# A two-layer recurrent block on one core: the high half of x1 moved a step ahead, the fp32 state moved to PSUM

## The chip, the cores and the metric

The kernel runs on one core of a Trainium2 chip. The metric is the device time of one execution in microseconds; the number given is the median over several runs. The engines are TensorE (PE: matrix products, PEld: its weight loads), VectorE (DVE), ScalarE (ACT), GpSimd (POOL) and SyncE (SP, which here only issues DMAs). Each engine works through its own instructions in order, and they meet through semaphores.

## What is computed

The input is x with 32 sequences of 64 steps and 256 features. There are two layers, and each adds to x the output of a feed-forward part that is fed by a recurrence over the 64 steps.

```python
# layer 0
gate  = sigmoid(h @ Wh.T + z_t @ Wz.T + b);  h = tanh(h * leak + gate * z_t)
x1    = x + experts(hs)          # 8 experts, the best 2 per token
# layer 1
h     = tanh(x1_t @ Wx + b + h @ Wh)
out   = x1 + bitlinear(gelu(bitlinear(hs, w1)), w2)   # ternary weights, 8-bit rows
```

In bitlinear each row of the activations is scaled by 127 over its largest absolute value and rounded; the weights are -1, 0 or 1 times a scale.

## The kernel before, in words

There are 2048 tokens in order of time, 128 to a tile, so that one tile holds four steps of the recurrence (32 sequences each) and there are 16 tiles. Float32 numbers that go into TensorE are split into two fp16 numbers, a high and a low one (the rest), and a product is made of three: high by high, low by high, high by low.

The program has three stages: the first recurrence (to about 125 us), 39 tiles of expert work (to about 286 us), and the second recurrence, in which the change lies. In the third stage every engine runs its own function tanh_tile(k, par) for tile k, with par = k % 2. Within it, four steps s = 0 to 3 follow one another, and behind the recurrence's part of each step stand pieces of other tiles' work. The order is written out by hand; nothing is scheduled by the program.

One step of the recurrence goes round three engines:

- TensorE (recur, L779 to L797): eight products with h_hi of the step before (L788), for which it waits for h2_ready; then it waits for lo2 and makes four with h_lo (L795). The sum stands in bank 0 or 1, on top of the input's projection.
- ScalarE (L731, L732): tanh twice from that bank, once as fp16 into h_hi and once as fp32 into h32, a tile in SBUF.
- VectorE (L1669): h_lo = h32 - h_hi.

The other pieces of a tile on VectorE, in the order in which they stand: after step 0 quantiser_hidden of tile k-3 (L1652, L1653; it releases GpSimd), write_out of tile k-5 (L1659), x1_high of tile k+2 (L1599: the high half of x1, 128x256, fp32 to fp16), peak_input of k-1 (L1625); after step 1 scale_input (L1630 to L1633), x1_low of k+2 (L1603: x1 minus its high half), combine_first of k+3 (L1586); after step 2 peak_hidden (L1638) and combine_second of k+3 (L1591); after step 3 floor, peak and scale_hidden (L1643, L1638, L1647). combine_first and combine_second make x1 out of two gathered rows of the experts' output. In tiles 0 and 1 ("early") the pieces for x1 stand elsewhere.

GpSimd does for each tile k quantise_hidden(k-3) (L535, 128x1024 from SBUF to SBUF, once quantiser_hidden is done) and then the two gathers for tile k+4 (L519), an indirect DMA each, which combine_first(k+4) waits for a tile later.

TensorE puts behind its steps: x1_transposed(k+1) (L1058, into bank 3), token_major(k-1) (bank 2) and half of hidden(k-2) after step 0; the other half and half of down_quantised(k-4) (L1111, bank 6) after step 1; half of the projection of x1 and hq_transposed after step 2; xq_transposed, the other half of the projection and of down_quantised after step 3.

Tiles 8 to 11 run in a loop on VectorE, tiles 6 to 13 on TensorE and ScalarE; the others are written out. In a loop the addresses and the values waited for are worked out in registers.

x1's two halves have one buffer, x1_s (L169), of which x1_high(t) may only overwrite the high half when x1_transposed(t-1) has read it.

## Time and profile before

| what | value |
|---|---|
| median of 3 runs | 392.41 us (390.03 to 393.56) |
| profiled execution | 392.09 us, span 390.1 us |
| PE busy | 327.8 us (84%) |
| DVE busy | 272.2 us (70%) |
| ACT busy | 232.7 us (60%) |
| POOL busy | 214.0 us (55%) |

The span is what the profile covers; the execution's own time lies 2.0 us above it. A busy share says little here, since the three stages have different limits. Starts are counted from the span's start. An instruction's duration can be longer than the time for which it keeps its engine: the next one on the same engine often starts a little before it ends.

### The profile page before, as it was taken

To read this page: it belongs to the slowest core of one execution; us is meant where nothing else is said; L and a number is where in the kernel's file an instruction comes from. 1 tells how busy PE (TensorE), PEld (TensorE's weight loads), DVE (VectorE), ACT (ScalarE), POOL (GpSimd) and SP (SyncE) were. 2 spreads that over 40 slices of the span, in tenths; PEclk is the share of its full clock that TensorE was granted. 3 is DMA by queue.
4 is the path that set the end of the run, shared out by engine and by line. 5 is a ranking of instruction groups with operands and counts; after the bars stand their busy time and mean duration, and the time that the engine had idled before them with its cause. 6 is when DMAs were issued, how large, how long until landed. Compare 5 with 4: busy or idle time off the path is not lost.

```text
span 390.1 us, 11984 instructions
## 1 busy us (share of the span) xinstructions
PE 327.8 (84%) x3816; PEld 231.3 (59%) x3817; DVE 272.2 (70%) x922; ACT 232.7 (60%) x733; POOL 214.0 (55%) x203
## 2 busy tenths in 40 slices
PE   2687777777577789999999999999987999999962
PEld 1444444444353357767777777777675777877841
DVE  5545555567996279587597878544456999999870
ACT  2356656565446446565656565565545878777871
POOL 5659999999804354454444745653115555562220
PEclk9999999998965699999999999999996999999998
DMA  8992185461592133222323332334213122221001
GB/s 209 201 396 103 42 297 188 160 244 64 193 337 75 29 124 89 66 86 68 90 64 91 90 89 73 96 82 79 69 39 97 32 83 69 81 67 41 29 29 40
DMA packets 22536, 42.95 MB, mean 110 GB/s; under 512 B 3986, under 2 KB 14610, under 8 KB 21604
## 3 DMA queue, kind: packets, MB, share of 16 engines
q0 software_dynamic: 6560, 23.17, 19.7%
q1 hardware_dynamic: 15664, 19.31, 15.7%
q8 instruction: 21, 0.34, 0.4%
q14 instruction: 15, 0.12, 0.1%
q10 hardware_dynamic: 276, 0.01, 0.0%
HBM read 28.97 MB, written 13.50 MB: 109 GB/s over the span
## 4 chain that ended last, share of the span: by engine, by line
PE 46%; DVE 14%; ACT 5%; issue 3%; DMA 2%; POOLq 0%; DVEq 0%; POOL 0%; ACTq 0%
PE bank L996 13%; PE bank L972 13%; PE bank L959 4%; PE bank L984 4%; DVE peak L1638 2%; PE bank L950 2%; DVE wrec L1599 2%; DVE h_lo L1669 1%; PE bank L952 1%; PE bank L1094 1%; PE bank L788 1%; PE bank L795 1%; DVE z_lo L1659 1%; PE bank L1111 1%; ACT z_hi L706 1%
## 5 line engine op out<-in xcount | busy, mean ns | idle before, releaser
L497 POOL DMA_INDIRECT xs<-hs_rows,row_of_slot x39 | 37.0, 948 | 72.3 <-PE bank L952 55.7
L788 PE MATMUL bank<-h_hi,wrec_hi 128*128 128x32 f16 x512 | 43.7, 181 | 29.3 <-ACT h_hi L595 27.8
L788 PEld LDWEIGHTS bank<-h_hi,wrec_hi 128*128 128x128 f16 x512 | 34.3, 97 | 56.0 <-ACT h_hi L595 49.6
L972 PE MATMUL bank<-wup_s,xt 128*128 x234 | 64.4, 385 | 0.0
L996 PE MATMUL bank<-wdn_s,wrec 128*128 x468 | 57.8, 273 | 0.3 <-ACT wrec L641 0.3
L996 PEld LDWEIGHTS bank<-wdn_s,wrec 128*128 128x128 f16 x468 | 45.2, 98 | 14.6 <-issue 1.1
L1492 DVE TENSOR_TENSOR wrec<-bank,wrec 128x512 f16<-128x512 f32 x39 | 27.0, 691 | 35.2 <-ACT wrec L641 34.8
L519 POOL DMA_INDIRECT z_lo<-y_rows,slot_i x32 | 31.1, 970 | 27.5 <-issue 26.4
L500 POOL DMA_INDIRECT gs<-gate_rows,row_of_slot x39 | 37.4, 958 | 11.9 <-issue 11.6
L1231 DVE TENSOR_TENSOR_SCAN bank<-bank,terms 128x128 f32<-128x128 f32 x64 | 27.6, 431 | 22.5 <-ACT bank L591 20.6
L788 PE MATMUL bank<-h_hi,wrec_lo 128*128 128x32 f16 x512 | 42.2, 178 | 0.0
L795 PE MATMUL bank<-h_lo,wrec_hi 128*128 128x32 f16 x512 | 33.9, 181 | 6.9 <-DVE h_lo L1669 6.0
L635 ACT ACTIVATE z_lo<-bank 128x256 f32<-128x256 f32 x39 | 15.0, 383 | 41.1 <-PE bank L996 41.1
L535 POOL TENSOR_SCALAR z<-z_hi,quant 128x1024 f16<-128x1024 f32 x16 | 17.9, 1118 | 38.8 <-DVE quant L1652 38.8
L649 ACT ACTIVATE xt<-bank 128x512 f16<-128x512 f16 x39 | 23.3, 597 | 19.2 <-PE bank L952 19.2
L788 PEld LDWEIGHTS bank<-h_hi,wrec_lo 128*128 128x128 f16 x512 | 32.7, 98 | 2.2 <-issue 0.3
L595 ACT ACTIVATE h_hi<-bank 128x64 f16<-128x64 f32 x64 | 14.3, 223 | 28.5 <-DVE bank L1231 28.5
L972 PEld LDWEIGHTS bank<-wup_s,xt 128*128 128x128 f16 x234 | 23.2, 99 | 11.9 <-issue 1.6
L795 PEld LDWEIGHTS bank<-h_lo,wrec_hi 128*128 128x128 f16 x512 | 21.7, 98 | 14.2 <-DVE h_lo L1669 7.1
L591 ACT ACTIVATE bank<-bank 128x64 f32<-128x64 f32 x64 | 13.3, 208 | 25.2 <-PE bank L795 20.6
L641 ACT ACTIVATE wrec<-bank 128x512 f16<-128x512 f32 x39 | 23.3, 598 | 8.2 <-PE bank L984 6.7
L1251 DVE TENSOR_TENSOR h_lo<-bank,h_hi 128x64 f16<-128x64 f32 x64 | 14.4, 225 | 17.4 <-ACT bank L596 15.8
(245 smaller groups left out, 964.1 us busy)
## 6 DMA issues: line engine op xcount, KB each, us to landing
y_rows<-z_lo SPq DMA_DIRECT2D x39, 128.0 KB, 1.8
stage<-wup POOLq DMA_DIRECT2D x2, 2048.0 KB, 10.8
gate_rows<-ga_s SPq DMA_DIRECT2D x16, 256.0 KB, 3.0
stage<-wdn POOLq DMA_DIRECT2D x2, 2048.0 KB, 10.5
stage<-wb SPq DMA_DIRECT2D x2, 1024.0 KB, 14.0
hs_rows<-hs_out SPq DMA_DIRECT2D x16, 128.0 KB, 2.3
stage<-w POOLq DMA_DIRECT2D x2, 1024.0 KB, 7.5
stage<-x_tm POOLq DMA_DIRECT2D x1, 2048.0 KB, 15.0
```

Of the source, the lines that this page charges most:

```text
L497: pool.indirect_dma_start(out=xs[par][:, :], out_offset=None, in_=hs_dram[0:tokens, :], in_offset=bass.IndirectOffsetOnAxis(ap=row_of_slot ...
L500: pool.indirect_dma_start(out=gs[par][:, 0:R], out_offset=None, in_=ga_dram[0:tokens * E, :], in_offset=bass.IndirectOffsetOnAxis(ap=row_o ...
L519: pool.indirect_dma_start(out=(ya, yb)[c][par][:, :], out_offset=None, in_=y_dram[0:tiles * P, :], in_offset=bass.IndirectOffsetOnAxis(ap= ...
L535: pool.tensor_scalar(hq[:, :], hid[par][:, :], quant2[par][:, :], ROUND, ALU.mult, ALU.add).then_inc(hq_ready, 1)
L641: sc.activation(act_t[:, 0, :, :].rearrange("p k t -> p (k t)"), bank[(7, 3)[par]][:, :], ACT.Copy).then_inc(at_hi_r, 1)
L649: sc.activation(xt[par][:, :, :, :].rearrange("p a k t -> p (a k t)"), bank[0][:, 0:D].bitcast(F16), ACT.Copy).then_inc(xt_ready, 1)
L788: mm(fm(par)[:, ft, cols], w[:, m, kt, fcols], h_hi[pp][:, kt, pcols], start=False, stop=True, skip_group_check=True)
L795: ins = mm(fm(par)[:, ft, cols], wrec_hi[:, m, kt, fcols], h_lo[pp][:, kt, pcols], start=False, stop=True, skip_group_check=True)
L972: ins = mm(bank[4 + par][:, :], xt[par][:, b, kt, :], w_slice(wup_s, a, kt, e), start=kt == 0 and n == 0, stop=kt == KT - 1 and n == 2)
L996: ins = mm(bank[6][:, 0:D], act_t[:, a, ft, :], w_slice(wdn_s, b, ft, e), start=n == 0, stop=n == len(todo) - 1)
L1231: ve.tensor_tensor_scan(flat(v[:, :, :, :]), flat(gate[:, :, :, :]), flat(terms[:, par, s]), 0.0, ALU.mult, ALU.add).then_inc(v_ready, 1)
L1492: ve.tensor_tensor(act_t[:, 1, :, :].rearrange("p k t -> p (k t)"), bank[(7, 3)[par]][:, :], act_t[:, 0, :, :].rearrange("p k t -> p (k t) ...
```

## The change

The fp32 state no longer goes into an SBUF tile. ScalarE writes it into 64 columns (256 to 319) of a PSUM bank, and VectorE reads it there: bank 3 for steps 1 to 3, bank 6 for step 0, and bank 2 for step 0 of tile 0. What TensorE writes into these banks in this stage lies in columns 0 to 255.

x1's halves get a second buffer, x1_second, and the parity of the tile picks one. With it, x1_high for tile k+3 stands at the end of tile k, after step 3, where x1_high for tile k+2 stood after step 0 before. It now waits for x1_transposed of two tiles back. x1_low stays where it was, as do tiles 2 and 3, whose two halves are made in tiles 0 and 1; tile 4's high half is made at the end of tile 1.

```diff
--- before.py
+++ after.py
@@ -115,7 +115,7 @@
         h_lo = [sb(f"h_lo{i}", [P, KT, P], F16) for i in range(2)]
         warm = sb("warm", [P, 3])
         h0 = sb("h0", [P, KT, BATCH])
-        h32 = sb("h32", [P, KT, BATCH])
+        x1_second = sb("x1_second", [P, 2, D], F16)
         hs_out = [sb(f"hs_out{i}", [P, 2 * D], F16) for i in range(2)]
         ga_s = [sb(f"ga_s{i}", [P, E * R]) for i in range(2)]
         sq = sb("sq", [P, E * R])
@@ -166,7 +166,8 @@
         act_t = free_w[:, F:2 * F].bitcast(F16).rearrange("p (a k t) -> p a k t", a=2, k=FT)
 
         xa = free_w[:, 2 * F:2 * F + D]
-        x1_s = free_w[:, 2 * F + D:2 * F + 2 * D].bitcast(F16).rearrange("p (a d) -> p a d", a=2)
+        x1_s = [free_w[:, 2 * F + D:2 * F + 2 * D].bitcast(F16).rearrange("p (a d) -> p a d", a=2),
+                x1_second[:, :, :]]
         x1t = free_w[:, 2 * F + 2 * D:2 * F + 3 * D].bitcast(F16).rearrange("p (a k t) -> p a k t", a=2, k=KT)
 
         peak = sb("peak", [P, 4])
@@ -218,6 +219,10 @@
 
         def fm(b, n=KT):
             return bank[b][:, 0:n * P].rearrange("p (k t) -> p k t", k=n)
+
+        def state(k, s):
+            b = 3 if s else 2 if isinstance(k, int) and k == 0 else 6
+            return bank[b][:, D:D + KT * BATCH].rearrange("p (k b) -> p k b", k=KT)
 
         def fm16(b, n):
             return bank[b][:, 0:n * P // 2].bitcast(F16).rearrange("p (k t) -> p k t", k=n)
@@ -729,7 +734,7 @@
                         cols = slice(s * BATCH, (s + 1) * BATCH)
                         sc.wait_ge(pre2, n + 1)
                         sc.activation(h_hi[par][:, :, cols], fm(par)[:, :, cols], ACT.Tanh)
-                        sc.activation(h32[:, :, :], fm(par)[:, :, cols], ACT.Tanh).then_inc(h2_ready, 1)
+                        sc.activation(state(k, s), fm(par)[:, :, cols], ACT.Tanh).then_inc(h2_ready, 1)
                     if isinstance(k, int) and (k, s) == (0, 0):
                         store_tile(STILES - 1, (STILES - 1) % 4)
                     if isinstance(k, int) and (k, s) == (1, 3):
@@ -1049,18 +1054,18 @@
                 expert = experts()
                 expert_tile(2 * i + 3, 1, expert, 0)
                 expert_tile(2 * i + 4, 0, expert, 1, 2 * i + 5)
-            def x1_transposed(t):
+            def x1_transposed(t, par):
                 pe.wait_ge(x1_split, t + 1)
                 if live(t - 1):
                     pe.wait_ge(x1t_ready, t)
                 at = 1 if isinstance(t, int) and t == 0 else 3
                 for c in range(2 * KT):
                     ins = nc.tensor.transpose(fm16(at, 4)[:, c, :],
-                                              x1_s[:, c // KT, (c % KT) * P:(c % KT + 1) * P], ident[:, :])
+                                              x1_s[par][:, c // KT, (c % KT) * P:(c % KT + 1) * P], ident[:, :])
                 ins.then_inc(x1t_mm, 1)
 
             expert = experts()
-            x1_transposed(0)
+            x1_transposed(0, 0)
             expert_tile(STILES - 2, 1, expert, 0)
             expert_tile(STILES - 1, 0, expert, 1)
             transposed_act(STILES - 1, 0)
@@ -1124,7 +1129,7 @@
                         down(STILES - 1, expert(1))
                     if s == 0:
                         if live(k + 1):
-                            x1_transposed(k + 1)
+                            x1_transposed(k + 1, 1 - par)
                         if live(k - 1):
                             if isinstance(k, int) and k == TILES:
                                 pe.wait_ge(lo2, STEPS)
@@ -1591,16 +1596,15 @@
                 ve.scalar_tensor_tensor(row_of(t), yb[par][:, :], mixw[:, 1, bass.ds(t, 1)], xa[:, :],
                                         ALU.mult, ALU.add).then_inc(x1_ready, 1)
 
-            def x1_high(t):
-                if isinstance(t, int):
-                    dve.wait_ge(x1_ready, t + 1)
-                if live(t - 1):
-                    dve.wait_ge(x1t_mm, t)
-                ve.tensor_scalar(x1_s[:, 0, :], row_of(t), 1.0, None, ALU.mult).then_inc(x1_hi_r, 1)
-
-            def x1_low(t):
+            def x1_high(t, par):
+                dve.wait_ge(x1_ready, t + 1)
+                if live(t - 2):
+                    dve.wait_ge(x1t_mm, t - 1)
+                ve.tensor_scalar(x1_s[par][:, 0, :], row_of(t), 1.0, None, ALU.mult).then_inc(x1_hi_r, 1)
+
+            def x1_low(t, par):
                 dve.wait_ge(x1_hi_r, t + 1)
-                ve.tensor_tensor(x1_s[:, 1, :], row_of(t), x1_s[:, 0, :], ALU.subtract).then_inc(x1_split, 1)
+                ve.tensor_tensor(x1_s[par][:, 1, :], row_of(t), x1_s[par][:, 0, :], ALU.subtract).then_inc(x1_split, 1)
 
             for j in range(29, STILES):
                 expert_tile(j, j % 2)
@@ -1609,15 +1613,15 @@
                     combine_first(0, 0)
                     combine_second(0, 0)
                 if j == 31:
-                    x1_high(0)
-                    x1_low(0)
+                    x1_high(0, 0)
+                    x1_low(0, 0)
                 if j == 36:
                     combine_first(1, 1)
                     combine_second(1, 1)
                 if j == STILES - 2:
-                    x1_high(1)
+                    x1_high(1, 1)
                 if j == STILES - 1:
-                    x1_low(1)
+                    x1_low(1, 1)
             act_low(STILES - 1, 0)
 
             def peak_input(t):
@@ -1666,15 +1670,13 @@
                         n = SPT * k + s
                         cols = slice(s * BATCH, (s + 1) * BATCH)
                         dve.wait_ge(h2_ready, n + 1)
-                        ve.tensor_tensor(h_lo[par][:, :, cols], h32[:, :, :], h_hi[par][:, :, cols],
+                        ve.tensor_tensor(h_lo[par][:, :, cols], state(k, s), h_hi[par][:, :, cols],
                                          ALU.subtract).then_inc(lo2, 1)
                     if s == 0:
                         if live(k - 3):
                             quantiser_hidden(k - 3, 1 - par)
                         if live(k - 5):
                             write_out(k - 5, 1 - par)
-                        if live(k + 2) and not early:
-                            x1_high(k + 2)
                         if live(k - 1):
                             peak_input(k - 1)
                     if s == 1:
@@ -1684,14 +1686,13 @@
                             combine_first(k + 2, par)
                             combine_second(k + 2, par)
                         if live(k + 2) and not early:
-                            x1_low(k + 2)
+                            x1_low(k + 2, par)
                         if live(k + 3) and not early:
                             combine_first(k + 3, 1 - par)
                     if s == 2:
                         if early:
-                            x1_high(k + 2)
-                        if early:
-                            x1_low(k + 2)
+                            x1_high(k + 2, par)
+                            x1_low(k + 2, par)
                         if live(k - 2):
                             peak_hidden(k - 2, par, 0)
                         if live(k + 3) and not early:
@@ -1704,6 +1705,8 @@
                         if early and k == 1:
                             combine_first(4, 0)
                             combine_second(4, 0)
+                        if live(k + 3) and not (early and k == 0):
+                            x1_high(k + 3, 1 - par)
 
             for k in range(8):
                 tanh_tile(k, k % 2)
```

VectorE, the written-out tile 7 of the second recurrence, from the end of tile 6 on, before. Here stage1 holds the rows of x1, wrec the buffer of x1's halves, and the digit of h_lo and h_hi is the tile's parity.

```order
L1638 TENSOR_REDUCE peak2<-z_hi 128x1
L1647 SCALAR_TENSOR_TENSOR peak2<-peak2,c_inv127 128x1
L1669 TENSOR_TENSOR h_lo1<-h32,h_hi1 128x2x32
L1652 RECIPROCAL quant20<-peak2 128x1
L1653 TENSOR_SCALAR deq2<-peak2,wscale 128x1
L1659 SCALAR_TENSOR_TENSOR z_lo<-bank6,deq2,stage1 128x256
L1599 TENSOR_SCALAR wrec<-stage1 128x256
L1625 TENSOR_REDUCE peak<-bank2 128x1
L1669 TENSOR_TENSOR h_lo1<-h32,h_hi1 128x2x32
```

The same place now:

```order
L1642 TENSOR_REDUCE peak2<-z_hi 128x1
L1651 SCALAR_TENSOR_TENSOR peak2<-peak2,c_inv127 128x1
L1603 TENSOR_SCALAR x1_second<-stage1 128x256
L1673 TENSOR_TENSOR h_lo1<-bank6,h_hi1 128x2x32
L1656 RECIPROCAL quant20<-peak2 128x1
L1657 TENSOR_SCALAR deq2<-peak2,wscale 128x1
L1663 SCALAR_TENSOR_TENSOR z_lo<-bank6,deq2,stage1 128x256
L1629 TENSOR_REDUCE peak<-bank2 128x1
L1673 TENSOR_TENSOR h_lo1<-bank3,h_hi1 128x2x32
```

The instruction that makes the high half (L1599, now L1603) has moved from behind write_out to ahead of step 0's h_lo, and h_lo reads a bank in place of h32. ScalarE has the same instructions in the same order; only where its second tanh goes is changed.

## Rows read from the trace of the kernel before

**Rows 1.** One stretch: length, busy us of PE PEld DVE ACT POOL, clock, DMA share.
```profile
314.00:330.20 16.20, 14.78 (x277) 12.77 (x275) 15.99 (x57) 13.26 (x46) 9.22 (x9) 1.00 0.27 80
```

**Rows 2.** The chain of waits: start, length, what.
```profile
291.80 2.74 DMA z_lo<-y_rows,slot_i
...
314.56 1.00 DVE wrec L1599
```

**Rows 3.** Timeline of VectorE: start, duration (us), line, operation, tiles, shapes.
```profile
319.22 0.23 DVE L1669 TENSOR_TENSOR h_lo<-h,h_hi 128x64 f16<-128x64 f32 x1
...
319.94 1.08 DVE L1599 TENSOR_SCALAR wrec<-stage 128x256 f16<-128x256 f32 x1
...
320.94 0.41 DVE L1625 TENSOR_REDUCE peak<-bank 128x1 f32<-128x256 f32 x1
...
321.26 0.21 DVE L1669 TENSOR_TENSOR h_lo<-h,h_hi 128x64 f16<-128x64 f32 x1
...
321.76 0.42 DVE L1603 TENSOR_TENSOR wrec<-stage,wrec 128x256 f16<-128x256 f32 x1
...
322.10 0.48 DVE L1586 SCALAR_TENSOR_TENSOR wrec<-z_lo,mixw,stage 128x256 f32<-128x256 f32 x1
...
324.68 0.22 DVE L1669 TENSOR_TENSOR h_lo<-h,h_hi 128x64 f16<-128x64 f32 x1
```

**Rows 4.** The same timeline, GpSimd.
```profile
319.75 1.12 POOL L535 TENSOR_SCALAR z<-z_hi,quant 128x1024 f16<-128x1024 f32 x1 [1.81 <-DVE quant L1652]
...
322.42 0.98 POOL L519 DMA_INDIRECT z_lo<-y_rows,slot_i  x1 [0.31 <-issue]
```

**Rows 5.** All instructions of one line: ns min/median/max, first and last start.
```profile
L1599 DVE TENSOR_SCALAR wrec<-stage x16: 284/778/1080, 257.4 to 358.5; 128x256 f16<-128x256 f32 x12, 128x256 f16 x4
```

**Rows 6.** VectorE (and GpSimd once), first steps of tiles, in order of time.
```profile
303.95 0.22 DVE L1669 TENSOR_TENSOR h_lo<-h,h_hi 128x64 f16<-128x64 f32 x1
...
304.45 1.12 POOL L535 TENSOR_SCALAR z<-z_hi,quant 128x1024 f16<-128x1024 f32 x1 [3.31 <-DVE quant L1652]
...
305.03 0.62 DVE L1669 TENSOR_TENSOR h_lo<-h,h_hi 128x64 f16<-128x64 f32 x1
...
313.76 0.23 DVE L1669 TENSOR_TENSOR h_lo<-h,h_hi 128x64 f16<-128x64 f32 x1
...
330.19 0.23 DVE L1669 TENSOR_TENSOR h_lo<-h,h_hi 128x64 f16<-128x64 f32 x1
...
352.32 0.23 DVE L1669 TENSOR_TENSOR h_lo<-h,h_hi 128x64 f16<-128x64 f32 x1
...
363.13 0.23 DVE L1669 TENSOR_TENSOR h_lo<-h,h_hi 128x64 f16<-128x64 f32 x1
```

**Rows 7.** Waits of TensorE's weight loads, 300 to 372 us: total, times, longest (us).
```profile
PEld bank L795 <- DVE h_lo L1669: 4.8, 10, 0.6
...
PEld bank L1111 <- issue: 3.6, 11, 0.7
```

**Rows 8.** Timeline of TensorE's products, columns as in rows 3; in brackets idle time before.
```profile
320.27 0.60 PE L1111 MATMUL bank<-w_q,z 128*128 128x256 f16 x4
...
321.53 0.27 PE L795 MATMUL bank<-h_lo,wrec_hi 128*128 128x32 f16 x4 [0.47 <-DVE h_lo L1669]
...
323.38 0.60 PE L1111 MATMUL bank<-w_q,z 128*128 128x256 f16 x4
...
324.02 0.25 PE L795 MATMUL bank<-h_lo,wrec_hi 128*128 128x32 f16 x4
```

**Rows 9.** All instructions of four lines, columns as in rows 5.
```profile
L1669 DVE TENSOR_TENSOR h_lo<-h,h_hi x64: 207/221/619, 286.2 to 371.7; 128x64 f16<-128x64 f32 x64
...
L1251 DVE TENSOR_TENSOR h_lo<-bank,h_hi x64: 217/225/230, 11.8 to 124.3; 128x64 f16<-128x64 f32 x64
...
L732 ACT ACTIVATE h<-bank x64: 218/219/254, 286.0 to 371.4; 128x64 f32<-128x64 f32 x64
...
L596 ACT ACTIVATE bank<-bank x64: 219/219/221, 11.5 to 124.0; 128x64 f32<-128x64 f32 x64
```

## The prediction

> **What bounds the kernel now.** The change touches the second recurrence alone, so I read the stage table for the stretch in which it runs evenly. From 314.0 to 330.2 us VectorE is busy for 15.99 of 16.20 us, TensorE's products for 14.78, ScalarE for 13.26, and the granted clock is 1.00, the upper of its two levels (2.4 GHz), so the clock explains nothing there [rows 1]. VectorE is full. In the chain of waits the making of x1's high half stands with 1.00 us a tile [rows 2].
>
> The timeline of one tile shows what that is. Tile 6 runs on VectorE from its step-0 h_lo at 319.22 to the next tile's at 324.68: **5.46 us**. In it L1599 takes 1.08 us and keeps the engine for 1.00 (the next instruction starts at 320.94) [rows 3]. The same instruction takes 0.28 us at its shortest; the median is 0.78, the longest 1.08 [rows 5]. It ends at 321.02. GpSimd's quantise_hidden runs from 319.75 to 320.87 [rows 4], so L1599 began under it and ended 0.15 us behind it: it waited for GpSimd and did its work afterwards. The h_lo at 305.03 tells the same: 0.62 us in place of a median of 0.22, ending at 305.65, while GpSimd's operation runs from 304.45 to 305.57 [rows 6, 9]. Both instructions read and write SBUF only. What reads PSUM does not stretch: 64 h_lo of the first recurrence, which read their fp32 state from a bank, took at most 0.230 us [rows 9], although GpSimd is busy there much of the time.
>
> This is what the Trainium skill, page "SBUF — State Buffer", section "Who interferes with whom", states: VectorE and GpSimd share a port pair, and whichever comes second is blocked to the end of the other's instruction, if VectorE's has two SBUF inputs or is a scalar operation in a two-port mode. By that rule a state in PSUM leaves h_lo free; the trace agrees, with 0.62 us against at most 0.23.
>
> Who waits for VectorE? TensorE's weight loads stand 4.8 us in all, 10 times, for h_lo [rows 7], once a tile: the step-1 h_lo stands behind L1599. That is what can come back.
>
> **Part 1, x1_high after step 3.** It now stands after scale_hidden and ahead of the next tile's step-0 h_lo. GpSimd starts only after quantiser_hidden, which comes after that h_lo, and ends with its second gather at 322.42 + 0.98 = 323.40, or 4.18 us after the tile's start at 319.22 [rows 3, 4]. The new place is at 4.4 to 4.6 us in the shortened tile, so x1_high meets nothing and keeps VectorE for 0.28 - 0.08 = 0.20 us (1.08 kept it for 1.00). VectorE's sum for a written-out tile: 5.46 - 1.00 + 0.20 = **4.66 us**.
>
> TensorE is then the bound. Its L795 of step 2 starts at 321.53, after waiting. Its predecessor L1111 starts at 320.27, and where nothing is late L795 follows such an L1111 by 324.02 - 323.38 = 0.64 us, so it would start at 320.91 [rows 8]. TensorE loses 0.62 us a tile and without that needs 5.46 - 0.62 = **4.84 us**. I take 4.87, since small joints between three engines in order never close fully. What is late next: TensorE's own row of work, then h_lo of step 0 behind the moved x1_high (VectorE has 4.84 - 4.66 = 0.18 us of slack a tile to hide that).
>
> The five written-out tiles (5, 6, 7, 12, 13) last 330.19 - 313.76 + 363.13 - 352.32 = 27.24 us [rows 6]. Five times 4.87 is 24.35: **gain 2.9**.
>
> In VectorE's loop, tiles 8 to 11 last 352.32 - 330.19 = 22.13 us, 5.53 each [rows 6]. Register work puts L1599 later under the same GpSimd operation, so it costs less: the median 0.78 [rows 5], 0.70 of the engine. VectorE's sum becomes 5.53 - 0.70 + 0.20 = 5.03, which is above TensorE's 4.84 and so is the bound; with the register work of the loop's turn not spread evenly I take 5.1. 22.13 - 4 x 5.1: **gain 1.7**. The moved instruction takes its register work along.
>
> **Part 2, the state in PSUM.** Tiles 3 and 4 last 313.76 - 303.95 = 9.81 us, 4.9 each, and in each the step-1 h_lo waits for GpSimd (0.62 - 0.22 = 0.40) [rows 6]. That goes; part of it is hidden behind ScalarE and TensorE, which are near their own limit at 4.84. Bounds 0 and 0.8 for the two; I take **0.4**. In tiles 14 and 15 the same stretch is hidden already: nothing. From tile 5 on, this part is what makes part 1 pay: without L1599 ahead of it, the step-1 h_lo would start at about 320.4 and meet GpSimd's operation (to 320.87) itself.
>
> The price: h_lo from a bank takes 0.225 against 0.221 us at the median, 64 times 4 ns is 0.3 us; bounds from the extremes are nothing and 0.230 - 0.207 = 23 ns, 1.5 us [rows 9]. I take 0.3, as the medians are of the same shape. ScalarE's second tanh takes 0.219 us into SBUF as into PSUM [rows 9]: nothing. TensorE writes other columns of bank 3 after step 0, when the state is in bank 6, and bank 6 after steps 1 and 3, when it is in bank 3, so they do not meet.
>
> A rule speaks against this part: the Trainium skill, "VectorE: DVE Perf Modes", section on the TRN2 errata, gives a fixed cost of 58 cycles from SBUF and 120 from PSUM. An estimate from that page: 62 cycles at 0.96 GHz are 65 ns, 4.1 us over 64 steps, and the time would be 391.5 us; the medians above, 4 ns apart, do not bear it out.
>
> **Small edits.** Scale_input's one-column operations come earlier, into the end of GpSimd's operation. No row shows such an operation meeting it; between nothing and the 0.3 us a tile until GpSimd is done, I take nothing, with the 0.18 us of slack as cover. x1_low (L1603, two SBUF inputs) follows 0.50 us behind the step-1 h_lo [rows 3]; that is now at about 320.45 + 0.50 = 320.95, just past 320.87. Uncovered, either of them would cost up to 0.3 us for 9 tiles, 2.7 us. The second buffer adds no instruction and the waits of x1_high are met long before.
>
> **Sum.** 2.9 + 1.7 + 0.4 - 0.3 = 4.7 us. It fits the 4.8 us that TensorE waits [rows 7], which is an upper bound of another kind (0.05 us is hidden in each of the 10, so about 5.3), less what the loop keeps. The profiled execution took 392.09 us (span 390.1) and would become 387.4. The median of the runs is 392.41, 0.3 above it, so I forecast **387.7 us**.
>
> **Rivals.**
> - *The next bound comes sooner.* TensorE's loads for L1111 stand 3.6 us, 11 times, after no releaser that the view can name [rows 7]; some of it can be the wait for write_out, which does not get earlier against TensorE. With tiles of 5.15 us, 363.13 - 313.76 = 49.37 becomes 46.35: 3.0, less 0.3, gives 389.7. For it: tiles 3 and 4 last 4.9 with one stretched h_lo; against: 0.62 us of pure standing in each tile. 25%.
> - *The PSUM state costs 23 ns a step*, on the loop of TensorE, ScalarE and VectorE: 1.2 us more, 388.9. The fp32 tanh and h_lo of the first recurrence speak against it. 9%.
> - *The stretch stays with the instruction*, wherever it stands, or scale_input and x1_low inherit it in full: no gain, about 392. Against: 0.28 us is reached in several tiles of this same stage, and all stretched ones end with GpSimd. 6%.
> - *The gathers become late, and it is slower.* The tile gets shorter and combine_first(k+4) comes earlier in it, while GpSimd's gathers keep their place. The second gather starts 322.42 - 319.22 = 3.20 us into a tile and lands 2.74 us after its start where the chain shows it [rows 2, 4], at 5.94. combine_first is now at 2.88 us of a tile (322.10) and would be at about 2.05 of the next, 6.9 after the same origin: 1.0 us to spare where 2.4 were. It decides from a landing of 4.4 us on: at 5.0 us, 3.20 + 5.0 - 2.05 makes a tile 6.15 long, 0.65 more than now for the nine tiles, 398 us, and each wait holds the step-2 h_lo behind it. Against: 2.74 measured. 5%.
>
> The forecast has 52%; the last 3% are for more than that: joints that close fully and L1599's stretch gone in tiles where I count nothing, about 386.
>
> **The numbers.** A difference of under 1% (3.9 us) is what a measurement of this kernel can hardly tell from no change; its runs lie 0.9% apart. Faster means below 388.5. My case lies 0.8 us under that, with an uncertainty of about 1 us, so four fifths of its 52%, plus a little of the first rival, plus the 3%, and a part of the second: 0.51. Slower only by the last rival and by accidents: 0.06. The rest, 0.43, is within 1%. The range reaches from 386.0 (TensorE's 5.3 us and the full 0.8 of tiles 3 and 4 come back, no price) to 391.5 (the first two rivals, and the 2.7 us of scale_input and x1_low on top of the forecast); beyond it are the third and the fourth.
>
> **What would show it.** x1_high (L1603 by the new line numbers) at about 0.28 us in all tiles; no h_lo over 0.25 us; tiles 5 to 7, 12 and 13 at 4.8 to 4.95 us, 8 to 11 at 5.0 to 5.2; TensorE's wait for h_lo near 1 us in place of 4.8; VectorE with idle time in tiles 5 to 7. I am wrong if x1_high is still stretched, if x1_low or scale_input ends with GpSimd's operation, if TensorE waits elsewhere for as long, or if combine_first waits for a gather.

## The result, and the profile after

| | before | after |
|---|---|---|
| median of 4 runs | 391.67 us (390.03 to 393.56) | 386.28 us (385.06 to 387.11) |
| ratio, 95% interval | | 0.9874 [0.9836, 0.9912] |
| profiled execution | 392.09 us, span 390.1 | 385.06 us, span 383.0 |
| third stage, from its first h_lo to the span's end | 390.1 - 286.24 = 103.9 us | 383.0 - 283.58 = 99.4 us |

The change makes the kernel 1.3% faster: 5.4 us by the medians, where 4.7 were forecast. The two profiled executions differ by 7.0 us, but 286.24 - 283.58 = 2.7 of those arose before the third stage, in code that the change leaves alone but for the buffer of tile 1's halves; over all the executions traced here, but for four on a chip of which more is said below, that stage begins between 283.6 and 287.2 us whichever kernel runs. So the profiles are compared by the third stage alone: 4.4 us.

First x1's high half. All instructions of its line, now L1603 (ns: shortest, median, longest), one row for each of the two buffers:

```profile
L1603 DVE TENSOR_SCALAR wrec<-stage x8: 284/286/294, 254.8 to 346.5; 128x256 f16<-128x256 f32 x6, 128x256 f16 x2
L1603 DVE TENSOR_SCALAR x_second<-stage x8: 283/287/289, 277.5 to 351.3; 128x256 f16<-128x256 f32 x6, 128x256 f16 x2
```

The longest is 0.29 us, where [rows 5] had a median of 0.78 and a longest of 1.08. The same view for h_lo (now L1673) and for ScalarE's second tanh (now L737), which answers to [rows 9]:

```profile
L1673 DVE TENSOR_TENSOR h_lo<-bank,h_hi x64: 209/224/227, 283.6 to 364.5; 128x64 f16<-128x64 f32 x64
...
L737 ACT ACTIVATE bank<-bank x64: 218/218/254, 283.3 to 364.2; 128x64 f32<-128x64 f32 x64
```

No h_lo is stretched any more, and the state in PSUM costs 224 - 221 = 3 ns an h_lo and nothing on ScalarE. VectorE's timeline of tile 5, from the end of tile 4 to tile 6's first h_lo, and GpSimd's beside it (start, duration in us, line; what is in brackets is idle time before):

```profile
312.06 0.29 DVE L1603 TENSOR_SCALAR x_second<-stage 128x256 f16<-128x256 f32 x1
312.26 0.22 DVE L1673 TENSOR_TENSOR h_lo<-bank,h_hi 128x64 f16<-128x64 f32 x1
...
313.31 0.23 DVE L1673 TENSOR_TENSOR h_lo<-bank,h_hi 128x64 f16<-128x64 f32 x1
313.45 0.14 DVE L1634 TENSOR_SCALAR peak<-peak 128x1 f32<-128x1 f32 x1
...
313.82 0.42 DVE L1607 TENSOR_TENSOR x_second<-stage,x_second 128x256 f16<-128x256 f32 x1
...
317.01 0.22 DVE L1673 TENSOR_TENSOR h_lo<-bank,h_hi 128x64 f16<-128x64 f32 x1
```

```profile
312.78 1.12 POOL L540 TENSOR_SCALAR z<-z_hi,quant 128x1024 f16<-128x1024 f32 x1 [2.51 <-DVE quant L1656]
314.17 0.97 POOL L524 DMA_INDIRECT z_lo<-y_rows,slot_i  x1 [0.27 <-issue]
```

GpSimd's operation covers 312.78 to 313.90. Under it now stand h_lo of step 1 (one operand in PSUM) and scale_input's one-column operation, and both have their usual length. The high half is made at 312.06, in the gap before. The tile lasts 317.01 - 312.26 = 4.75 us, where [rows 3] had 5.46.

What is full now? Three stretches of the stage (length; busy us of PE, PEld, DVE, ACT, POOL; clock), to be read against [rows 1]:

```profile
312.00:326.00 14.00, 14.00 (x273) 12.00 (x271) 13.73 (x57) 13.26 (x44) 9.53 (x9) 1.00 0.26 78
326.00:346.00 20.00, 19.57 (x370) 16.30 (x367) 19.12 (x77) 17.93 (x61) 13.03 (x12) 1.00 0.26 78
346.00:356.00 10.00, 10.00 (x200) 8.66 (x197) 9.15 (x38) 9.51 (x33) 2.51 (x3) 1.00 0.13 41
```

In the written-out tiles (first and third row) TensorE's products are busy without a gap, where they were busy for 14.78 of 16.20 us; VectorE has some idle time. In VectorE's loop (second row) TensorE still stands a little. TensorE is the bound that came next.

Tile by tile, each from its step-0 h_lo to the next tile's:

| tiles | before | after | forecast |
|---|---|---|---|
| 3 and 4 | 9.81 us | 10.76 us | 9.41 us |
| 5, 6, 7, 12, 13 (written out) | 27.24 us | 23.78 us | 24.35 us |
| 8 to 11 (loop) | 22.13 us | 20.08 us | 20.4 us |

Two groups gained more than forecast and one lost. That the three changes add up to 4.6 us here, close to the 4.7 forecast, is chance: tiles 5 to 13 gave 0.9 us more than forecast, and tiles 3 and 4 came out 1.35 us longer. The loss stands in one row of tile 4:

```profile
309.49 0.48 DVE L1591 SCALAR_TENSOR_TENSOR wrec<-z_lo,mixw,stage 128x256 f32<-128x256 f32 x1 [1.45 <-DMA z_lo<-y_rows,slot_i]
```

That is combine_first, and it waits for a gather. The chain of waits shows that gather and another, three tiles on (start, length):

```profile
304.67 4.80 DMA z_lo<-y_rows,slot_i
...
320.19 3.67 DMA z_lo<-y_rows,slot_i
323.88 0.48 DVE wrec L1591
```

The first lands 4.80 us after its start. The second lands 3.67 us after its start, about 0.2 us after combine_first could have begun, and tile 7 lasts 4.88 us in place of 4.76. That is the last of the prediction's rivals, with 1.45 us at one tile and 0.1 us at another. TensorE's waits for its weight loads between 297 and 372 us (total, times, longest) say the same, against [rows 7]:

```profile
PEld bank L1116 <- issue: 4.8, 13, 0.7
PEld bank L800 <- DVE h_lo L1673: 1.6, 2, 1.4
```

The 4.8 us for h_lo, forecast to become about 1, became 1.6, of which 1.4 is the one behind the gather.

### The profile page after: what moved, and what is told of

Read it like the earlier page. It is cut to its first block, busy times and chain, and to the rows that moved or that the text cites. A ratio compares the mean times of both kernels' runs of the same rounds, so it can differ in the third digit from the quotient of the medians.

```text
span 383.0 us, 11985 instructions
## 1 busy us (share of the span) xinstructions
PE 321.4 (84%) x3816; PEld 228.1 (60%) x3817; DVE 265.5 (69%) x922; ACT 233.7 (61%) x733; POOL 215.8 (56%) x203
## 4 chain that ended last, share of the span: by engine, by line
PE 49%; DVE 9%; ACT 4%; DMA 4%; issue 3%; POOL 1%; POOLq 0%; DVEq 0%; ACTq 0%
PE bank L1001 13%; PE bank L977 13%; PE bank L964 4%; PE bank L989 4%; DMA z_lo<-y_rows,slot_i 3%; PE bank L955 2%; PE bank L1116 2%; DVE peak L1642 2%; PE bank L1099 2%; PE bank L793 2%; PE bank L957 1%; PE bank L800 1%; DMA gs<-gate_rows,row_of_slot 1%; DVE z L1381 1%; ACT z_hi L711 1%
## 5 line engine op out<-in xcount | busy, mean ns | idle before, releaser
L977 PE MATMUL bank<-wup_s,xt 128*128 x234 | 63.1, 379 | 0.0
L524 POOL DMA_INDIRECT z_lo<-y_rows,slot_i x32 | 32.3, 1008 | 27.5 <-issue 26.4
L1508 DVE TENSOR_TENSOR terms<-terms,bank 128x512 f32<-128x512 f32 x39 | 26.4, 678 | 0.0
```

The lines of the kernel that those rows point to most:

```text
L524: pool.indirect_dma_start(out=(ya, yb)[c][par][:, :], out_offset=None, in_=y_dram[0:tiles * P, :], in_offset=bass.IndirectOffsetOnAxis(ap= ...
L977: ins = mm(bank[4 + par][:, :], xt[par][:, b, kt, :], w_slice(wup_s, a, kt, e), start=kt == 0 and n == 0, stop=kt == KT - 1 and n == 2)
L1508: ve.tensor_tensor(act[:, :], silu[:, :], bank[4 + par][:, :], ALU.mult).then_inc(act_r, 1)
```

## The experiments

Twelve runs were made, of eight kernels, four runs at a time on one chip. "Before" in each group is the kernel before on that same chip.

### First chip: the parts taken apart, and a surprise

**e1_move_only** has the moved x1_high with its second buffer, and leaves the state in SBUF:

```diff
+        h32 = sb("h32", [P, KT, BATCH])
...
         def state(k, s):
-            b = 3 if s else 2 if isinstance(k, int) and k == 0 else 6
-            return bank[b][:, D:D + KT * BATCH].rearrange("p (k b) -> p k b", k=KT)
+            return h32[:, :, :]
```

> The new x1_high and its second buffer, but the fp32 state in SBUF as before. My theory (what stretches is any VectorE instruction that reads and writes SBUF under GpSimd's quantise_hidden): x1_high 0.28 us everywhere, but the step-1 h_lo now starts at about 1.2 us of a tile, under GpSimd's operation (0.53 to 1.65), and takes 0.55 to 0.65 us in each tile from 3 to 15. Written-out tiles 4.85 to 5.0 us in place of 4.76 with the whole change; time 1 to 2 us above the whole change. Rival (the state's place is worth nothing): h_lo at most 0.25 us in tiles 5 to 13 and the same time as the whole change.

**e2_psum_only** is the kernel before with only the state moved to PSUM:

```diff
-  h32 = sb("h32", [P, KT, BATCH])
...
+  def state(k, s):
+      b = 3 if s else 2 if isinstance(k, int) and k == 0 else 6
+      return bank[b][:, D:D + KT * BATCH].rearrange("p (k b) -> p k b", k=KT)
...
-  sc.activation(h32[:, :, :], fm(par)[:, :, cols], ACT.Tanh).then_inc(h2_ready, 1)
+  sc.activation(state(k, s), fm(par)[:, :, cols], ACT.Tanh).then_inc(h2_ready, 1)
...
-  ve.tensor_tensor(h_lo[par][:, :, cols], h32[:, :, :], h_hi[par][:, :, cols],
+  ve.tensor_tensor(h_lo[par][:, :, cols], state(k, s), h_hi[par][:, :, cols],
```

> The fp32 state in PSUM, but one buffer for x1's halves and x1_high where it was. My theory: x1_high still takes 0.8 to 1.1 us in tiles 5 to 13, whose length stays at 5.4 to 5.5; no h_lo over 0.25 us; a gain of 0.5 us from tiles 3 and 4 only, so 0 to 1 us faster than before. Rival (a PSUM operand costs VectorE 65 ns): h_lo 0.28 us and 1 to 3 us slower than before.

**e3_after** is the changed kernel itself.

> The whole change again, for a second profile. If the one wait of 1.45 us for a gather in tile 4 of the first profile belongs to the schedule, combine_first in tile 4 waits here too, 0.5 to 1.7 us, and tile 4 takes 5.3 to 6.3 us. If it was chance, tile 4 takes 4.7 to 4.8 us. The time within 1 us of 386.3.

**e4_half_quantise** is the kernel before with a GpSimd operation of half the width:

```diff
-  pool.tensor_scalar(hq[:, :], hid[par][:, :], quant2[par][:, :], ROUND, ALU.mult, ALU.add
+  n = HID if t == 0 else HID // 2
+  pool.tensor_scalar(hq[:, 0:n], hid[par][:, 0:n], quant2[par][:, :], ROUND, ALU.mult, ALU.add
```

> The kernel before, but from tile 1 on GpSimd quantises only the first half of the hidden row (512 of 1024 columns; the output is not the reference's), so its operation ends about 0.5 us sooner. If x1_high waits for GpSimd's operation, it ends 0.15 us behind it as before, takes about 0.5 to 0.6 us in place of 1.08 in the written-out tiles, and each of tiles 5 to 13 gets about 0.4 to 0.5 us shorter: 4 us faster than before. Rival (the stretch belongs to the instruction): x1_high keeps 0.8 to 1.08 us and the time stays.

| kernel | median | ratio to before | tiles 5 to 11, each | tiles 12, 13 |
|---|---|---|---|---|
| before | 416.62 us (25 runs) | | | |
| e1, move only | 418.57 us | 1.006 [1.0017, 1.0104] | 6.45 to 6.75 us | 5.10, 4.82 us |
| e2, PSUM only | 415.87 us | 0.9983 [0.9947, 1.002] | 6.36 to 6.68 us | 5.46, 5.35 us |
| e3, both | 415.29 us | 0.9982 [0.9945, 1.0018] | 6.42 to 6.73 us | 4.76, 4.63 us |
| e4, half the width | 412.4 us | 0.9879 [0.9842, 0.9916] | 5.96 to 6.27 us | 5.03, 4.93 us |

On this chip the kernel before takes 25 us more than it took elsewhere, and the change gives nothing. Its tiles 5 to 11 last about 6.5 us whichever part is in. Tiles 12 and 13 have the known lengths, and in them the gain is there in full: 5.46 and 5.35 (e2) against 4.76 and 4.63 (e3). What differs is that tiles 12 and 13 start no gathers. Part of the 25 us arises before the third stage: e2's kernel, run again on the third chip as e11, has a span of 391.0 us there against 414.1 here, and its third stage starts at 286.6 us there against 297.6 here. In e3's trace, ScalarE and GpSimd in one tile:

```profile
349.34 0.22 ACT L736 ACTIVATE h_hi<-bank 128x64 f16<-128x64 f32 x1 [1.57 <-remote]
```

```profile
345.04 1.12 POOL L540 TENSOR_SCALAR z<-z_hi,quant 128x1024 f16<-128x1024 f32 x1 [2.61 <-DVE quant L1656]
346.42 0.97 POOL L524 DMA_INDIRECT z_lo<-y_rows,slot_i  x1 [0.27 <-issue]
347.70 1.17 POOL L524 DMA_INDIRECT z_lo<-y_rows,slot_i  x1 [0.30 <-issue]
351.48 1.12 POOL L540 TENSOR_SCALAR z<-z_hi,quant 128x1024 f16<-128x1024 f32 x1 [2.61 <-DVE quant L1656]
```

Once a tile, at step 3, ScalarE stands before a tanh, with a releaser that the view can only call "remote", and goes on 1.64 us after the tile's second gather began. It stood so 10 times in e3, for 17.0 us in all (the longest 3.1), and never in the traces from other chips. Eight of the ten stands, from tile 3 on, end 1.5 to 1.8 us after the second gather began; those in tiles 1 and 2 end 0.6 and 2.1 us after it. The tanh releases h_lo, the next tile's quantiser_hidden, then GpSimd's next operation, the gathers and the next stand: a ring of 351.48 - 345.04 = 6.44 us in which most of VectorE's work is hidden. That the gather is what the tanh waits for is read from the distance in these eight and from tiles 12 and 13; no run shows it. A gain on VectorE can hardly show while that ring is the bound. What ScalarE waits for there was not found, so for the size of the change this chip says nothing. Its traces still tell lengths of instructions. In e4, VectorE and GpSimd in tile 12:

```profile
376.53 0.65 DVE L1600 TENSOR_SCALAR wrec<-stage 128x256 f16<-128x256 f32 x1
```

```profile
376.34 0.69 POOL L536 TENSOR_SCALAR z<-z_hi,quant 128x512 f16<-128x512 f32 x1 [2.78 <-DVE quant L1653]
```

GpSimd's operation is 1.12 - 0.69 = 0.43 us shorter and so is the stretched x1_high, 1.08 - 0.65 = 0.43 (e2's takes 1.08 in the same tile on this chip), though nothing of x1_high was edited. It ends 0.15 us behind GpSimd's, as in [rows 3, 4]. So the stretch is the rest of GpSimd's operation, and not the instruction's own. That e4 is faster even here fits the ring: GpSimd's operation is a part of it, and 0.43 us in each of tiles 5 to 11 would be 3.0 of the 4.2 us; against e2 these seven tiles are 2.6 us shorter. That e1 is the slowest is not explained by the ring. The h_lo that is stretched in e1 is that of step 1, which is not on the path described, and tiles 5 to 11 take 45.96 us in e1 against 45.77 in e3; 0.5 us more stands in tiles 12 and 13, and the rest of the 3.3 us between the medians has no cause that the traces show.

The expectations on the lengths of instructions held in the main: x1_high takes at most 0.30 us in e1 and a median of 0.78 us in e2, the step-1 h_lo takes 0.38 to 0.67 us in tiles 4 to 15 of e1 (0.24 in tile 3), and no h_lo takes over 0.23 us in e2 and e3. Those on the lengths of tiles 5 to 11 failed, and so did the time of e3. Whether tile 4's wait for a gather belongs to the schedule e3 can't say, since the ring sets that tile's length too (6.59 us).

### Second chip: the same parts where the ring does not bind

**e5_before_profile** is the kernel before, once, for its trace on this chip.

> The kernel before once more, for a profile on the same chip as the runs beside it. On the chip of the four runs so far the tiles in which GpSimd gathers (1 to 11) took about 6.4 us with the change and without x1_high moved, and only tiles 12 and 13 were as short as in the first profiles. If that is the chip's doing, this kernel has it too on such a chip: tiles 5 to 11 at 6.3 to 6.5 us, 12 and 13 at 5.4; on a chip like the first, 5.46 to 5.7 us and 5.4. If the change brings it, tiles 5 to 11 take 5.5 us on either.

**e6_after_again** is the changed kernel, and **e7_move_only_again** is e1's kernel.

> The whole change once more. On a chip like the first: tiles 5 to 13 at 4.6 to 5.1 us and 1.0 to 1.5% faster than before. On a chip like the last: tiles 5 to 11 at 6.4 to 6.6 us, held by ScalarE's first tanh of step 3, which starts about 1.6 us after the start of the second gather, and 0 to 0.5% faster.

> The new x1_high with the fp32 state in SBUF. On a chip like the first: the step-1 h_lo takes 0.5 to 0.66 us in tiles 4 to 15, tiles 5 to 13 at 4.9 to 5.2 us, 1 to 2 us above the whole change and 3 to 4 us below before. Rival (the stretch of h_lo is covered): the same time as the whole change within 0.5 us.

**e8_gather_first** is the changed kernel with another order on GpSimd in tile 3, the tile whose gathers came late in the profile after:

```diff
             def tanh_tile(k, par):
-                if live(k - 3):
+                if live(k - 3) and k != 3:
                     quantise_hidden(k - 3, 1 - par)
...
+                if k == 3:
+                    quantise_hidden(k - 3, 1 - par)
```

> The whole change, and in tile 3 alone GpSimd issues the two gathers for tile 7 ahead of quantise_hidden(0) instead of behind it (about 1.4 us sooner). If combine_first(7) in tile 4 waits for this gather by the schedule, its wait of 1.45 us shrinks to 0 to 0.3 us and the kernel is 0.5 to 1.5 us faster than the whole change. If that wait was chance, there is no difference, or a loss up to 0.5 us where hq_transposed(0) gets its input later.

| kernel | median | ratio to before | tiles 3, 4 | tiles 5 to 13, sum |
|---|---|---|---|---|
| before | 391.85 us (11 runs) | | 4.89, 4.92 us (e5) | 49.35 us (e5) |
| e6, after | 386.52 us | 0.986 [0.982, 0.9901] | 4.86, 4.64 us | 43.71 us |
| e7, move only | 387.77 us | 0.9892 [0.9858, 0.9926] | 5.09, 5.11 us | 45.93 us |
| e8, gathers first in tile 3 | 386.52 us | 0.9855 [0.9817, 0.9893] | 5.89, 5.79 us | 43.73 us |

e5 took 393.11 us, and its tiles are those of the first profile to within 0.03 us. e6 repeats the gain, 5.3 us, and has no wait for a gather in tile 4; between 307 and 359 us its chain of waits runs over TensorE, but for 334.9 to 339.1 us in VectorE's loop, where it goes over ScalarE and VectorE.

e7 shows what the move costs without the second part. VectorE and GpSimd in tile 5:

```profile
313.86 0.67 DVE L1673 TENSOR_TENSOR h_lo<-h,h_hi 128x64 f16<-128x64 f32 x1
```

```profile
313.34 1.12 POOL L540 TENSOR_SCALAR z<-z_hi,quant 128x1024 f16<-128x1024 f32 x1 [1.48 <-DVE quant L1656]
```

The step-1 h_lo, with both operands in SBUF, has taken x1_high's place under GpSimd's operation and ends with it (314.53 against 314.46). It is stretched to between 0.38 and 0.77 us in every tile from 3 to 15. Tiles 5 to 7 last 5.10 or 5.11 us in place of 4.76. Placing the state in PSUM is worth 45.93 - 43.71 = 2.2 us in tiles 5 to 13 of these two profiles. The medians differ by 1.25 us, with six runs each and intervals of the ratio that overlap, so the time alone hardly shows it. This is the rule of the Trainium skill, page "SBUF — State Buffer", section "Who interferes with whom", told twice by one instruction: with two SBUF inputs h_lo is held to the end of GpSimd's, with one of them in PSUM it is not.

In e8 the gathers are early and tile 4 has no wait for one. Since e6 has none either, e8 doesn't tell whether the order prevents it. But another wait has come, on TensorE, for the quantised rows that now come later:

```profile
307.62 0.62 PE L1110 MATMUL bank<-ident,z 128*128 128x128 f16 x8 [1.42 <-POOL z L540]
```

and behind it the granted clock fell (stretches as above; the clock is the third number from the right):

```profile
306.00:309.00 3.00, 1.58 (x32) 1.41 (x30) 1.89 (x6) 1.64 (x7) 1.48 (x2) 0.92 0.18 55
309.00:312.00 3.00, 3.00 (x40) 2.17 (x39) 1.98 (x9) 2.24 (x8) 1.12 (x1) 0.51 0.02 5
312.00:315.00 3.00, 3.00 (x59) 2.79 (x58) 2.77 (x12) 2.59 (x10) 1.92 (x2) 1.00 0.15 44
```

Tiles 3 and 4 together are 2.2 us longer than in e6. The traced execution is the slowest of e8's six (388.68 us), so this loss need not be in all of them. The medians are equal: this order is no better than the other.

### Third chip: the loop, the second part alone, and twice the load

**e9_after_control** is the changed kernel once more. **e10_vector_unrolled** has VectorE's tiles 8 to 11 written out, TensorE's and ScalarE's loops as they were:

```diff
-            for k in range(8):
-                tanh_tile(k, k % 2)
-            with dve.Fori(4, (TILES - 4) // 2) as i:
-                tanh_tile(2 * i, 0)
-                tanh_tile(2 * i + 1, 1)
-            for k in range(TILES - 4, TILES + 5):
+            for k in range(TILES + 5):
                 tanh_tile(k, k % 2)
```

> The whole change, as the control for the three beside it. On a chip like the first: 1.2 to 1.5% faster than before, tiles 5 to 7, 12 and 13 at 4.6 to 4.8 us, 8 to 11 at 4.9 to 5.1.

> The whole change with VectorE's loop over tiles 8 to 11 written out (the same instructions without register work). If VectorE's register work is what makes these tiles 0.25 us longer than their neighbours, they take 4.76 us and the kernel gains 0.9 to 1.1 us on the control. Rival (TensorE and ScalarE, which still loop over them, set 5.0 us): no difference.

**e11_psum_only_again** is e2's kernel.

> The fp32 state in PSUM alone. On a chip like the first: tiles 5 to 13 at 5.35 to 5.75 us as before (sum within 0.3 us of 49.4), x1_high 0.78 to 1.08 us in them, tiles 3 and 4 together 0.2 to 0.5 us shorter; the time 0 to 1 us below before. Then the parts' gains don't add up: part 1 alone gave 4 us, both 5.3.

**e12_quantise_twice** is the changed kernel with GpSimd's operation done twice, the first time into a spare region:

```diff
                 pool.sem_inc(waited, 1)
+                pool.tensor_scalar(act_s[:, :, :].rearrange("p a f -> p (a f)"), hid[par][:, :], quant2[par][:, :], ROUND, ALU.mult, ALU.add)
                 pool.tensor_scalar(hq[:, :], hid[par][:, :], quant2[par][:, :], ROUND, ALU.mult, ALU.add
```

> The whole change, with GpSimd quantising the hidden row twice (2.2 us in place of 1.12, from 0.53 to about 2.8 us of a tile), so that scale_input, x1_low and combine_first fall under it. Theory (an instruction is held if it has two SBUF inputs, or is a scalar operation in a two-port mode; a state in PSUM frees h_lo): h_lo stays at 0.22 us; peak_input and the other reductions stay; x1_low (two SBUF inputs) ends at the end of GpSimd's operation plus 0.1 to 0.4 us, taking up to 1.3 us; the one-column operations of scale_input are the open case: 0.14 us if free, up to 1.3 us if held. Rival (every VectorE instruction is slowed a little while GpSimd works in SBUF): all of them stretch by some per cent, none ends with GpSimd's.

| kernel | median | ratio to before | tile 4 | tiles 5 to 13, sum |
|---|---|---|---|---|
| before | 390.76 us (17 runs) | | | |
| e9, after | 385.98 us | 0.9884 [0.9849, 0.9919] | 5.52 us | 43.71 us |
| e10, after, VectorE written out | 385.74 us | 0.9852 [0.9819, 0.9885] | 4.65 us | 42.69 us |
| e11, PSUM only | 390.86 us (12 runs) | 0.9996 [0.9969, 1.0023] | 6.14 us | 49.27 us |
| e12, GpSimd twice | 403.01 us (1 run) | | 6.06 us | 53.9 us |

e10's tiles 8 to 11 last 4.75 to 4.77 us in place of 4.91 to 5.08, and TensorE's products have no gap there any more:

```profile
314.00:350.00 36.00, 36.00 (x693) 30.89 (x691) 35.48 (x145) 34.31 (x116) 22.29 (x21) 1.00 0.26 77
```

So what kept the loop's tiles above the others was the register work of VectorE's loop, 1.0 us in all. In the time this can't be seen: 0.9 to 1.1 us less than e9 was expected, the medians differ by 0.24 us and the means by 1.4, and each kernel's six runs spread over almost 4 us.

In e11 x1_high is stretched as in the kernel before (1.08 and about 0.78 us), no h_lo is, and the time is the time before: the second part alone gives nothing, to within 1 us. Its tile 3 is 0.4 us shorter than before (4.49 us), which tile 4 loses again by a late gather. So a late gather does not need the move. Tile 4's combine_first in e9, and in e11:

```profile
309.44 0.48 DVE L1591 SCALAR_TENSOR_TENSOR wrec<-z_lo,mixw,stage 128x256 f32<-128x256 f32 x1 [0.84 <-DMA z_lo<-y_rows,slot_i]
```

```profile
312.26 0.48 DVE L1589 SCALAR_TENSOR_TENSOR wrec<-z_lo,mixw,stage 128x256 f32<-128x256 f32 x1 [1.47 <-DMA z_lo<-y_rows,slot_i]
```

Of the traces from chips where the ring does not bind, this wait is in the profile after, e9, e11 and e12, and not in the profile before, e5, e6, e7, e8 and e10. Of the three traces in which x1_high is made at its old place one has it (e11), and of the three of the kernel after two have it: the same kernel has it in one execution and not in another. All four traces with the wait have the state in PSUM, as have three without it, and none of the four is from the second chip. These few traces don't tell whether either of the two matters.

In e12 GpSimd's two operations cover nearly all of step 1's pieces. VectorE and GpSimd in one tile:

```profile
323.66 0.23 DVE L1674 TENSOR_TENSOR h_lo<-bank,h_hi 128x64 f16<-128x64 f32 x1
323.80 0.14 DVE L1635 TENSOR_SCALAR peak<-peak 128x1 f32<-128x1 f32 x1
...
324.17 0.41 DVE L1608 TENSOR_TENSOR wrec<-stage,wrec 128x256 f16<-128x256 f32 x1
324.50 0.48 DVE L1592 SCALAR_TENSOR_TENSOR wrec<-z_lo,mixw,stage 128x256 f32<-128x256 f32 x1
```

```profile
322.96 1.12 POOL L540 TENSOR_SCALAR wrec<-z_hi,quant 128x1024 f16<-128x1024 f32 x1 [0.65 <-DVE quant L1657]
324.16 1.73 POOL L541 TENSOR_SCALAR z<-z_hi,quant 128x1024 f16<-128x1024 f32 x1
```

h_lo and the one-column operation run under the first of them at their usual length. All 16 one-column operations of L1635, 14 of them under a GpSimd operation, take 142 to 153 ns, and the longest h_lo of the 64 takes 226 ns. x1_low starts at 324.17, at the same time as GpSimd's second operation, with combine_first behind it, and then it is that operation which takes 1.73 us in place of 1.12: the holding goes both ways. In three tiles x1_low began 0.13 to 0.17 us after GpSimd's second operation; there x1_low took 1.23 to 1.25 us and GpSimd's operation its usual 1.12. What e12 costs over e9, 17.0 us by its single run, has mostly another place: TensorE waits for the quantised rows before hq_transposed (total, times, longest; in e9 such waits are 0.5 us in all):

```profile
PE bank L1109 <- POOL z L541: 13.9, 15, 1.3
```

## Why the prediction was right, and where its sizes were off

The forecast was 387.7 us, the median 386.28. Half of those 1.4 us is the base: a fourth run of the kernel before brought its median from 392.41 to 391.67. The other half is the gain, 5.4 us in place of 4.7.

**The mechanism is shown.** x1_high was held by GpSimd's operation: e4 shortened that by 0.43 us and x1_high followed by 0.43; at its new place it takes 0.29 us. h_lo was held for the same cause (e7 0.67 us against 0.227 at most in PSUM). TensorE is the next bound (14.00 of 14.00 us).

**Written-out tiles: 27.24 to 24.35 forecast, 23.78 measured.** TensorE's need of 4.84 us a tile was worked out from the single place where it stood longest [rows 8]; it is 4.75 us. The 0.03 us added for joints was not needed, and 0.09 us more came back. The trace shows where: one step later the products with h_lo were late as well. From the step's first product to the first of those with h_lo, before and after:

```profile
322.48 0.18 PE L788 MATMUL bank<-h_hi,wrec_hi 128*128 128x32 f16 x1
...
322.77 0.27 PE L795 MATMUL bank<-h_lo,wrec_hi 128*128 128x32 f16 x4
```

```profile
319.53 0.18 PE L793 MATMUL bank<-h_hi,wrec_hi 128*128 128x32 f16 x1
...
319.74 0.25 PE L800 MATMUL bank<-h_lo,wrec_hi 128*128 128x32 f16 x4
```

That is 0.29 us before and 0.21 after, and so in each of tiles 5 to 12 of the kernel before (0.28 or 0.29 us): the step-2 h_lo stood behind combine_first, which was late because x1_high was. [rows 1] would not have told: TensorE's products were idle for 1.42 us there in three tiles, 0.48 us each, less than the 0.62 us counted. Over five tiles these differences make about the 0.57 us.

**Loop tiles: 20.4 forecast, 20.08 measured.** VectorE's sum of 5.03 us a tile was right (5.02 on average), the allowance to 5.1 was not needed. e10 shows that the reason given, the loop's register work, is the right one.

**Tiles 3 and 4: 9.41 forecast.** Measured were 10.76 in the profile after, and 9.50 (e6), 10.15 (e9: 4.63 + 5.52) and 9.28 (e10). Without a late gather the 0.4 us is about right. The gather's wait is what the last rival said, and I gave too little weight to the row 2.74 us being one landing of many: here it was 3.67 and 4.80. The 4.4 us of the prediction are where a tile gets longer than it was before. A wait begins sooner: by the prediction's own figures at 2.74 + 1.0 = 3.7 us, and in the trace at 308.04 - 304.67 = 3.4 us, since combine_first could have begun at 308.04. It comes at one or two tiles and costs up to 1.5 us, not 0.65 us at each of nine.

**The price of PSUM** was 4 ns a step forecast and 3 ns measured, 0.2 us in all. The Trainium skill, "VectorE: DVE Perf Modes", section on the TRN2 errata, would have given 65 ns a step by an estimate from its 62 cycles; the medians 221 and 224 ns go against it in this use.

**The parts do not add.** By their medians the move alone gives 4.1 us (e7), PSUM alone nothing (e11: ratio 0.9996), both together 5.3 (e6). The prediction said that from tile 5 on the second part makes the first pay. That is right in kind and was given no number; it is 2.2 us in the profiles, 1.25 us in the medians. PSUM alone gains nothing in tiles 5 to 13, because x1_high at its old place is held to the end of GpSimd's operation and the step-1 h_lo stands behind it.

**The bounds were worked out loosely.** The lower edge, 386.0 us, is 392.09 - 5.3 - 0.8, from the profiled execution; from the median of 392.41, on which the forecast stands, it is 386.3, and the measured 386.28 lies on it. The upper edge does not come out of the terms named for it: 387.7 + 2.0 + 1.2 + 2.7 is 393.6, not 391.5. And the 5.3 us called an upper bound were none: between e5 and e6 tiles 5 to 13 alone got 49.35 - 43.71 = 5.6 us shorter. The 0.08 us a tile above are a part of this that [rows 7] does not count.

**Small edits at no cost**: scale_input under GpSimd's operation is free (0.14 us, also in e12). x1_low does pay if it falls under it whole (up to 1.25 us in e12), but in the kernel after it began 0.08 us before that end and took 0.42; the second buffer adds nothing that a trace shows.

Of the rivals, the next bound came later than the first one feared (5.15 us tiles; 4.75 measured). The PSUM rival and the one in which the stretch stays are refuted by the rows above. What I had not thought of is a chip on which the change is worth nothing: the bound of a stage read from one chip's profile need not be another's.

**What stays open:** what ScalarE waits for on the first chip; whether the gather is what ends that wait; and why a gather lands 2.7 us after its start at one place and 4.8 at another.

## What to carry to other kernels

When one instruction of VectorE takes two to four times its shortest time, lay GpSimd's timeline beside it: if it ends just behind a GpSimd operation, move it into GpSimd's idle stretch, and see to it that what slides into its old place is of a kind that is not held (an operand in PSUM, or one column). Work out the new tile from what the next engine needs in all, not from its one longest wait, and look for transfers whose consumer gets earlier while they do not.

## What the runs showed of the hardware that I had not expected

- A GpSimd operation can itself be held by VectorE's operations with two SBUF inputs: 1.73 us in place of 1.12 where they began together, and 1.12 where VectorE's began 0.13 to 0.17 us later (e12).
- The kernel before took 416.62 us on one chip and 390.76 to 391.85 in the other three groups of runs. Of the four traces from that chip, all with an edit or the change, e3's has ten waits on ScalarE whose releaser the view can't name, eight of which end 1.5 to 1.8 us after an indirect gather began.
- In e8, 1.42 us of standing before one TensorE instruction was followed by 3 us at a granted clock of 0.51, the lower level (1.2 GHz). In the profile after, TensorE's products were busy for only 0.88 of 2.00 us while it waited behind the gather, and the clock stayed at the upper level:

```profile
308.00:310.00 2.00, 0.88 (x21) 0.77 (x18) 0.55 (x3) 1.25 (x4) 1.65 (x2) 1.00 0.12 27
310.00:312.00 2.00, 1.83 (x38) 1.79 (x39) 1.96 (x7) 1.41 (x7) 0.27 (x1) 1.00 0.33 105
```
